# Attention layer with a gated MoE: the next batch's inputs split into halves before they are turned, and turned by DMA

## The reference, cut to what matters

```python
def layer(x, ctx):                       # x, ctx: (8, 512, 512) float32
    x = x + tanh(g_xattn) * cross_attention(layernorm(x), ctx)   # 16 heads of 32
    x = x + tanh(g_ffn) * moe(layernorm(x))   # router, top 2 of 8 experts, 512 -> 2048 -> 512
    return x

def cross_attention(query, ctx):
    Q = query @ Wq.T + bq;  K = ctx @ Wk.T + bk;  V = ctx @ Wv.T + bv
    attn = softmax(Q K^T / sqrt(32))          # per head, 512 x 512
    return (attn @ V) @ Wo.T + bo
```

## Time and profile before

| | |
|---|---|
| three runs | 1891.55, 1891.44, 1890.22 us; median 1891.44 us |
| profiled execution, its own time | 1890.38 us |
| its span in the trace | 1888.6 us, granted TensorE clock 0.974 of full speed in the mean |
| busy, of the span | TensorE 94%, VectorE 60%, ScalarE 41%, GpSimd 24% |

### The profile page before, as it was taken

The page is one execution under the profiler, slowest core; times in us unless marked ns, Lnnn a source line. Parts: engine busy times, 40 slices in busy tenths (PEclk is TensorE's granted clock), DMA queues, the critical chain, the costliest instruction groups (busy, mean ns, idle before and its releaser), DMA issues.

```text
span 1888.6 us, 30415 instructions
## 1 busy us (share of the span) xinstructions
PE 1778.4 (94%) x10826; PEld 923.5 (49%) x10826; DVE 1134.8 (60%) x2199; ACT 774.1 (41%) x1012; POOL 453.1 (24%) x424
## 2 busy tenths in 40 slices
PE   7999999999999999999814999999999999999996
PEld 4334243342423334243203767676666767676664
DVE  6777777778777777777677634435353635434330
ACT  4453634446353453634421516244351516244330
POOL 2322423223332322421211122111122122111102
PEclk9999999999999999999956999999999999999998
DMA  6313233131422413123022343415243343415201
GB/s 221 98 46 112 68 118 105 50 124 48 130 93 82 141 45 111 67 66 114 33 103 78 108 119 87 143 47 162 71 138 76 102 124 85 143 45 164 71 26 25
DMA packets 138206, 178.98 MB, mean 95 GB/s; under 512 B 45492, under 2 KB 86592, under 8 KB 134056
## 3 DMA queue, kind: packets, MB, share of 16 engines
q1 hardware_dynamic: 97192, 157.85, 25.1%
q0 software_dynamic: 40960, 20.41, 6.1%
HBM read 134.08 MB, written 43.63 MB: 94 GB/s over the span
## 4 chain that ended last, share of the span: by engine, by line
PE 84%; DVE 8%; issue 2%; ACT 2%; POOL 1%; DMA 1%; SPq 0%; DVEq 0%; ACTq 0%; POOLq 0%
PE psum L1533 22%; PE psum L1510 20%; PE psum L1324 7%; PE psum L1331 7%; PE psum L1315 6%; PE psum L1295 6%; PE psum L1305 6%; PE psum L1417 4%; PE psum L1342 3%; DVE mx L895 2%; PE psum L1224 2%; ACT osum L761 1%; DVE reached L1039 1%; PE psum L1481 1%; DVE x2hl L959 1%
## 5 line engine op out<-in xcount | busy, mean ns | idle before, releaser
L1533 PE MATMUL psum<-w,hT 128*123 128x512 f16 x1920 | 420.3, 379 | 0.0
L1510 PE MATMUL psum<-xgT,w 128*128 128x308 f16 (+1 forms) x3072 | 412.5, 295 | 0.8 <-DVE xgT L1140 0.8
L895 DVE TENSOR_REDUCE mx<-psum 128x1 f32<-128x512 f32 x512 | 331.2, 684 | 106.5 <-PE psum L1305 104.4
L1510 PEld LDWEIGHTS psum<-xgT,w 128*128 128x128 f16 x3072 | 298.9, 98 | 110.7 <-DVE xgT L1140 1.1
L1533 PEld LDWEIGHTS psum<-w,hT 128*123 128x123 f16 x1920 | 257.9, 135 | 148.8
L750 ACT ACTIVATE pt<-psum 128x1024 f32<-128x1024 f32 x256 | 259.1, 1021 | 166.4 <-PE psum L1315 165.8
L818 ACT ACTIVATE h<-psum,b1c 128x308 f32<-128x308 f32 (+1 forms) x256 | 117.8, 511 | 381.3 <-PE psum L1510 380.1
L1168 DVE TENSOR_TENSOR hT<-h,hT 128x615 f16<-128x615 f32 x128 | 102.5, 801 | 213.5 <-ACT hT L821 213.5
L653 POOL DMA_INDIRECT out_dram<-y,idx_now x40 | 99.3, 2483 | 498.6 <-DVE y L1203 265.6
L1295 PE MATMUL psum<-actT,wT 128*128 128x512 f16 x768 | 177.5, 379 | 2.0 <-DVE wT L882 2.0
L1305 PE MATMUL psum<-stk 96*128 96x512 f16 x512 | 171.0, 383 | 4.0 <-DVE mx L895 1.5
(11 more groups left out here) (186 smaller groups left out, 1610.1 us busy)
## 6 DMA issues: line engine op xcount, KB each, us to landing
stage<-in_L_ffn_W_dram SPq DMA_DIRECT2D x62, 1024.0 KB, 5.3
stk<-qk_rows SPq DMA_DIRECT2D x192, 128.0 KB, 2.5
qk_rows<-qks SPq DMA_DIRECT2D x64, 256.0 KB, 2.5
xin<-in_x_dram SPq DMA_DIRECT2D x8, 1024.0 KB, 5.2
cin<-in_ctx_dram SPq DMA_DIRECT2D x8, 1024.0 KB, 7.4
xres<-in_x_dram SPq DMA_DIRECT2D x8, 1024.0 KB, 5.6
out_dram<-xres SPq DMA_DIRECT2D x32, 256.0 KB, 2.1
x_split<-x2hl SPq DMA_DIRECT2D x32, 256.0 KB, 2.3
```

The lines of the kernel that those rows point to most:

```text
L895: v.reduce_max(mx[:, KT * t + qt:KT * t + qt + 1], ps, AX.X).then_inc(read, 1)
L1510: mm = t_.matmul(psum[:, (2 * m + ch) % 4, 0:c1 - c0], w1[:, wp, kt, m * P:(m + 1) * P], xgT[:, xp, kt, c0:c1], start=(kt == 0 and (wp, xp ...
L1533: mm = t_.matmul(psum[0:CP, Y_BANK[c], :], hT[:, hp, k, c * CP:(c + 1) * CP], w2[:, wp, k, :], start=(k == 0 and (hp, wp) == (0, 0)), stop ...
```

## The change

For the next batch, the inputs are now split with rows still on the partitions, and the halves are turned by DMA. `next_hl[n]` is float16 space for both halves, four tiles of rows by 1024 columns: `qk32` is used for x and `x2n` for the context. ScalarE makes the high halves (`next_hi`), context in slots 3 to 6 and x in slots 11 to 14; VectorE the low halves (`next_lo`), context in slots 3 to 6 and x in slots 16 to 19. SyncE issues four transposing DMAs of 128 rows x 1024 columns (256 KB) for the context behind the `mrow` DMAs of group 2 and four for x behind those of group 3. TensorE's turning and VectorE's splits remain for batch 0 alone. The pieces of the diff stand in this order: constants and space, SyncE (`inputs_turned`, `batch`), ScalarE, VectorE (`next_lo`, the slots, the end of the batch), TensorE (`queries_keys`, the slots).

```diff
+C_HI_SLOT, C_LO_SLOT, X_HI_SLOT, X_LO_SLOT = 3, 3, 11, 16
+C_TURN_GROUP, X_TURN_GROUP = 2, 3
...
+        next_hl = [a.rearrange("p t d -> p (t d)").bitcast(f16).rearrange("p (t d) -> p t d", t=KT)
+                   for a in (qk32[:, :, :], x2n[:, :, :])]
...
+            def inputs_turned(b, n):
+
+                sp.wait_ge(lo_ready[n], KT * b + KT)
+                settle(sp)
+                if n == 1:
+                    copied(sp, use, ("v", KT - 1), b)
+                    settle(sp)
+                for tt in range(KT):
+                    dst = actT[:, n, :, :, tt * P:(tt + 1) * P].rearrange("p a k s -> p (a k) s")
+                    sp.dma_start(dst, next_hl[n][:, tt, :], transpose=True).then_inc(act_in[n], 16)
+
             def batch(b, first, last):
                 if not last:
-
-                    sp.wait_ge(act_hi, 2 * KT * b + 2 * KT)
+                    if first:
+                        sp.wait_ge(act_hi, 2 * KT)
                     settle(sp)
                     sp.dma_start(xin[:, :, :], x_b[b + 1]).then_inc(x_in, 16)
                     sp.dma_start(cin[:, :, :], c_b[b + 1]).then_inc(c_in, 16)
...
+                    if not last and g == C_TURN_GROUP:
+                        inputs_turned(b, 1)
+                    if not last and g == X_TURN_GROUP:
+                        inputs_turned(b, 0)
...
+                def next_hi(n, tt):
+
+                    if n == 0:
+                        act.wait_ge(xn_ready, KT * b + (KT + tt + 1))
+                        act.wait_ge(qk_split, NQ * b + NQ)
+                    elif tt == 0:
+                        act.wait_ge(c_in, 16 * b + 32)
+                    s.activation(next_hl[n][:, tt, 0:D], (xn, cin)[n][:, tt, :], ACT.Copy,
+                                 scale=(1.0, SX)[n]).then_inc(hi_ready[n], 1)
...
                     if t >= LAG_B:
                         for tt in later_v(t):
                             values(tt)
+                    for n, slot in ((1, C_HI_SLOT), (0, X_HI_SLOT)):
+                        if not last and slot <= t < slot + KT:
+                            next_hi(n, t - slot)
                     if t in GROUP_END[:-1]:
...
+                def next_lo(n, tt):
+
+                    dve.wait_ge(hi_ready[n], KT * b + tt + 1)
+                    hl, src = next_hl[n][:, tt, :], (xn, cin)[n][:, tt, :]
+                    v.scalar_tensor_tensor(hl[:, D:2 * D], src, (1.0, SX)[n], hl[:, 0:D],
+                                           ALU.mult, ALU.subtract).then_inc(lo_ready[n], 1)
...
                     maxima(t, (2, 3))
-                    if not last:
-                        for i in act_tiles(t):
-                            inputs_split(b + 1, i // KT, i % KT)
+                    for n, slot in ((1, C_LO_SLOT), (0, X_LO_SLOT)):
+                        if not last and slot <= t < slot + KT:
+                            next_lo(n, t - slot)
...
+                if not last:
+                    dve.wait_ge(act_in[1], 16 * KT * b + 16 * KT)
                 for tt in range(KT):
                     normalise(1, tt, KT * b + tt, xres[:, tt, :], x2n[:, tt, :], x2n_ready)
...
-                    if m == 0:
+                    if m == 0 and first:
                         for kt in range(KT):
-                            copied(pe, act_use, ("actT", n, kt), b)
+                            copied(pe, pre, ("actT", n, kt))
+                    if m == 0 and not first:
+                        pe.wait_ge(act_in[n], 16 * KT * b)
...
-                    if not last_batch and s > UNITS:
-                        for i in act_tiles(s):
-                            inputs_transposed(b + 1, i // KT, i % KT)
...
-                    if not last_batch and s == UNITS:
-                        for i in act_tiles(s):
-                            inputs_transposed(b + 1, i // KT, i % KT)
```

More of the change, by code:

```diff
@@ L63, in later_v @@
     return [V_FIRST + j for j, slot in enumerate(V_SLOT) if slot == s]
-def act_tiles(s):
-    return [i for i in range(2 * KT) if min(UNITS + i, SLOTS - 1) == s]
+C_HI_SLOT, C_LO_SLOT, X_HI_SLOT, X_LO_SLOT = 3, 3, 11, 16
+C_TURN_GROUP, X_TURN_GROUP = 2, 3
 class Banks:
@@ L256, in batch_banks @@
                     banks.add("lg", 7)
-                if not last:
-                    for i in act_tiles(s):
-                        banks.add(("actT", i // KT, i % KT), (1, 0)[i % 2])
                 for qt in range(2, KT):
@@ L285, in use_before @@
             return use_last(key) if isinstance(b, int) and b == B else use_loop(key, b, back=1)
-        def act_use(key, b):
-            return pre(key) if isinstance(b, int) and b == 0 else use_loop(key, b, back=1)
         bank_full = [sem(f"bank_full{i}") for i in range(8)]
@@ L330, in layer_kernel @@
         act_hi = sem("act_hi")
+        hi_ready = [sem("x_hi_ready"), sem("c_hi_ready")]
+        lo_ready = [sem("x_lo_ready"), sem("c_lo_ready")]
+        act_in = [sem("x_turned"), sem("c_turned")]
         qk32_ready, qk_split = sem("qk32_ready"), sem("qk_split")
@@ L865, in _, with inputs_split @@
                     normalise(0, tt - 1, tt - 1, xin[:, tt - 1, :], xn[:, tt - 1, :], xn_ready)
[L867 to L873, removed]
+            def inputs_split(n, kt):
+                dve.wait_ge(act_hi, KT * n + kt + 1)
+                ps, read = read_by_last(pre, ("actT", n, kt))
                 v.scalar_tensor_tensor(actT[:, n, 1, kt, :], ps, (1.0, SX)[n], actT[:, n, 0, kt, :],
@@ L885, in _ @@
                     for kt in range(KT):
-                        inputs_split(0, n, kt)
+                        inputs_split(n, kt)
             dve.wait_ge(tgbo_ready, 2)
@@ L1233, in _, with inputs_transposed @@
                    v32[:, :, :], xres[:, :, :]]
-            def inputs_transposed(b, n, kt):
+            def inputs_transposed(n, kt):
                 if kt == 0:
-                    pe.wait_ge(*((xn_ready, KT * b + KT), (c_in, 16 * b + 16))[n])
-                dst, full = claim(pe, act_use, ("actT", n, kt), b)
+                    pe.wait_ge(*((xn_ready, KT), (c_in, 16))[n])
+                dst, full = claim(pe, pre, ("actT", n, kt))
                 transposes(dst, [(xn, cin)[n][:, tt, kt * P:(kt + 1) * P] for tt in range(KT)]).then_inc(full, 1)
@@ L1248, in _ @@
                     for kt in range(KT):
-                        inputs_transposed(0, n, kt)
+                        inputs_transposed(n, kt)
             for kt in range(KT):
```

## The result

The changed kernel took 1924.97 us in the median of four runs (1922.09 to 1926.07), the kernel before 1891.36 on the same chip. The ratio is 1.0177, with a 95% interval of 1.0164 to 1.0190: 33.6 us slower, where 27.1 were forecast (1918.5, range 1901 to 1948). The profiled execution took 1924.38 us.

A forecast was written before the change was run, and what follows sets the result against it. TensorE, busy 94% of the span, was taken as the bound, with VectorE as near in slots 3 and 4. 6.5 + 0.3 - 2.93 = 3.87 us a batch, 27.1 in seven, gave 1918.5 us, range 1901 to 1948.

The forecast's parts named there:

- The gain: Slots 16 to 22: TensorE loses 32 transposes in each of seven batches, 2.93 us a batch less.
- The chain in slots 3 to 6: VectorE's low halves wait for ScalarE's high halves, delaying statistics, maxima and TensorE's scores: 6.5 us a batch more.
- Slot 14: A high half of x on ScalarE delays the head group's copy that TensorE waits for: 0.3 us a batch.
- The turns: Transposing DMAs in SyncE's queue: taken as hidden, costing nothing; a little late 0.08, much later or clock falling 0.07.
- The limit: SyncE: the context's four turns may take 13.0 us, 3.25 each, before group 3's `mrow` makes anything wait.
- the worse end: SyncE's queue: turns issued piece by piece, 27 us a turn as an estimate from the skill; chance 0.03.
- VectorE's decoupling: Slots 3 and 4, rival: TensorE and VectorE, half a slot apart, absorb the wait; 1878 us, chance 0.09.
- price for the passes: VectorE's four low halves of 0.61 us where it is full, without the wait: 0.7 us a batch.
- the clock: TensorE, rival: clock falls in the new gaps, another 70 us, 1988; chance 0.07 together with turns much later.
- the sum: Whole batch: 6.5 + 0.3 - 2.93 = 3.87 us more a batch, 27.1 us in seven batches.

## Why the prediction was right

*The gain.* 2.93 us a batch, from batch 7 of the kernel before. The stretch measured 21.27 us after, as in batch 7. Shown.

*The chain in slots 3 to 6.* Forecast lateness of TensorE at slot 7's first product with the values: 5.76 us, slot 0 to there 34.1; measured 34.2 in the batches at full clock. VectorE's waits: about 2.4 forecast, 2.35 and 2.32 measured. TensorE's: 2.6 and 2.0 forecast, 2.42 and 1.98 measured; at slot 7 0.74 forecast, 0.67 measured. The high half took 0.63 us, where 0.60 was taken. Two details differ: VectorE's wait in slot 5 was forecast shorter and was 2.3 us, as in slots 3 and 4, and TensorE's small wait at slot 6 was forecast at 0.39 and was 0.29 (in batch 6 its scores start 0.72 us after the products ahead of them, 0.43 in the kernel before). Moving the producer one slot (47.8 us back), adding the pair alone (57.8 us lost) and moving the statistics out of the chain (1.9 us a batch) show the mechanism from three sides. That 3.87 met 3.88 is in part luck: the chain cost 6.56 and not 6.5, slot 14 0.25 and not 0.3, and the two errors cancel.

*Slot 14.* 0.3 us forecast; TensorE's wait for the copy went from 0.17 to 0.42, and moving the high halves took just this away.

*The turns.* Taken as hidden, and hidden. The limit was 13.0 us for four. They are issued 1.33 us apart, 5.4 us for the four, and each lands 3.3 us after its own issue, so all are in after 7.4 us. The run with six more turns puts the limit at 13.05. The trace does not agree with the worse end that the prediction worked out from the Trainium skill (DMA: Bandwidth & Descriptors, section Why a DMA increments its semaphore by 16 and not by 1, the column of previous generations, read with tiles of 256 bytes): 27 us of SyncE's time for a turn by that estimate, 1.33 measured. The Trainium skill's 261 GB/s (the same page, section Latency and other measured facts) gave an estimate of 1.0 us; 262,144 bytes every 1.33 us are 197 GB/s.

*The rivals.* VectorE's decoupling absorbed nothing; that rival would have given 1878 us, and it is what the kernel does once the wait is taken away (1877.2). Its price for the passes, 0.7 us a batch, was right (0.67).

*The term that was mis-sized is the clock.* It was a rival of its own, at 70 us for ten microseconds of half speed in every batch, and the forecast took it as nothing. Measured: 7.9 us over five of seven batches. Those 7.9, less the 1 us of the mixture of experts, are the whole difference between the 3.88 x 7 = 27.2 us of the sum and the 34.0 of the trace. The argument that 2.0 us of standing had been harmless once, before the first queries, was one sample of something that goes either way. In the kernel with the statistics ahead, 1.47 us did it in two batches and not in five. And at the very place of the argument, the stand of 2.0 to 2.1 us ahead of the first queries, which all ten profiled kernels have, the clock fell in one of the ten, that with two more turns; the same 48 matmuls, 10.52 us in the earlier trace rows, took 12.13:

```profile
28.40 12.13 PE L1336 MATMUL psum<-actT,wT 128*128 128x512 f16 x48 [1.99 <-DVE wT L911]
```

## What to carry to other kernels

When a step is split over two in-order engines, give the consumer a later slot than the producer: what counts is not the 0.6 us that the step takes but everything that stands ahead of the producer in its own order, here TensorE's filling at the end of the slot, and everything that stands behind the wait on the consumer. One number, a slot of 7 in place of 3, turned 1.8% slower into 1.0% faster. And price a wait on a TensorE that is nearly full at more than its length: after gaps of 1.5 to 2.4 us the clock fell in some batches and not in others, and in the changed kernel a batch in which it fell was 0.9 to 3.0 us longer for it.

## What the runs showed of the hardware

A transposing DMA of 128 rows by 1024 float16 (256 KB), with SBUF on both sides (the trace's DMA issues, with the median us from issue to landing; then the context's 28 turns, ns min/median/max on SyncE):

```profile
actT<-x2n SPq DMA_TRANSPOSE x28, 3.3
actT<-qk SPq DMA_TRANSPOSE x28, 3.3
```
```profile
L454 SPq DMA_TRANSPOSE actT<-x2n x28: 1265/1333/1363, 104.9 to 820.2; - x28
```

SyncE is held 1.33 us by each, where a plain store of the same size, to HBM, holds it 0.56 (four in 2.24 us). The packets under 512 bytes grew from 45,492 to 104,628, which is 1,056 for each of the 56 turns. None of it reached TensorE as long as the queue behind was not late: a batch with the low halves at slot 7 is 110.84 us, what the sum without the turns gives, and 110.85 with two turns more.

TensorE's clock fell after gaps of 2.4 and 2.0 us in five of seven batches of the changed kernel and in seven of seven of the kernel before with the halves added, after 1.5 and 1.0 us in two of seven, after 6.0 us and more in seven of seven, and in none of the seven in the kernel before or with the low halves at slot 7, whose gaps from slot 0 to the projection are at most 0.25 and 0.61 us. In the changed kernel it fell right after the first gap in four of the five batches, and only after the second in batch 3.
